# A depthwise 5x5 convolution on TensorE: stores issued by ACT, a reordered first channel, other waits on DVE

## The chip, the cores and the metric

One core of a Trainium2 chip runs the kernel. The metric is device time in microseconds (us) of one execution. The engines are TensorE (PE, with its weight loads shown as PEld), VectorE (DVE), ScalarE (ACT), GpSimd (POOL) and SyncE (SP). DMAs are issued here by SP and by ACT (their queues are shown as SPq and ACTq) and run on 16 DMA engines.

## The reference

The input x is 128 images of 55 x 55 pixels with 96 channels, float32. Each channel is convolved with its own 5 x 5 kernel, and the input is added:

```python
ch = x.shape[-1]
k = jnp.transpose(kernel, (1, 2, 0))[:, :, None, :]
y = lax.conv_general_dilated(x, k, window_strides=(1, 1), padding='SAME',
                             dimension_numbers=('NHWC', 'HWIO', 'NHWC'), feature_group_count=ch)
return x + y
```

Four of the 96 kernels are not zero in the given data, but the kernel computes all 96 alike.

## The kernel before, in words

**Layout.** The host turns x so that a channel is one array of 128 partitions by 3200 columns. The 55 x 55 image is cut into 5 x 5 squares of 11 x 11 pixels. Partition p is pixel p of a square (121 are used), and the columns run over strips (five columns of squares, j = 0 to 4), squares of a strip (top to bottom) and the 128 images. So one square of all images is a 121 x 128 block, and it is the stationary operand of a matmul. The moving operand is the channel's taps, spread out into a 121 x 225 matrix: from each of the 121 pixels to the 15 x 15 window that it reaches. The product, 128 images by up to 225 pixels, goes to PSUM. The 1 on the centre tap adds the input itself.

**Precision.** x and the taps are each split into a high part that TensorE takes exactly (float32r) and the rest. Three products make the result: x_low with the high taps, x_high with the high taps, x_high with the low taps. ACT makes x_high (`split_high`, L336 to L347, a copy with rounding), DVE or POOL subtracts to get x_low (`split_low`, L282 to L286). From channel 1 on, a channel is split in two pieces (LATER_PIECES, L116): strips 0 and 1, whose x_low DVE makes, and strips 2 to 4, whose x_low POOL makes. Channel 0 is split in five pieces, one a strip, all by DVE. The taps are split by DVE in batches of four channels, in three steps (`split_taps`, L243 to L268), and placed into the weights by one multiplication with a mask (`place_taps`, L270 to L280): by DVE for channel 0, by POOL for all others.

**Tiles.** A channel has 14 tiles (TILES, L60): in each of the strips 0 to 3 the squares (0), (1, 2) and (3, 4), in strip 4 the squares (0, 1) and (2, 3, 4). A tile has a PSUM bank of its own; there are 8, used in turn, so tile i waits until tile i - 8 is finished (`wait_bank`, L434 to L442; i runs on through the channels). A tile with one square (`alone`) takes two matmuls, since its third product is put beside the second in one instruction and lands in a part of the bank of its own. The others take three matmuls a square. That makes 71 matmuls in a channel.

**Finishing a tile.** Windows of neighbouring squares overlap by four pixels, the seam. ACT copies the pixels of a tile that no tile before has touched from PSUM to y_out (`copy_sums`, L349 to L354). DVE then adds what is left (`finish_sums`, L371 to L395): in an alone tile the low part of the same pixels (L381); where the tile has one above it, the four rows of seam (L386); where it has one to its left, the four columns of seam (L392), in an alone tile twice, for its high and its low part (L392, L395). Each addition counts up the semaphore y_step; `stepped(c, i)` is its value when tile i of channel c is done. Before L386 DVE waits until all steps of the tile before are complete (L384), and before L392 likewise (L391).

**Order on each engine.** The order is written out by hand. ACT (L356 to L367): issues the loads of start_in (the taps of channels 0 to 3, the unit kernel and the mask) and of the taps of batch 1, splits the five pieces of channel 0, then for each channel makes 14 copies, with the two splits of the next channel ahead of copies 0 and 3 (HIGH_AT, L119), in channel 0 ahead of copies 5 and 8. DVE (L397 to L420): zeroes the weights, splits and places the taps of channel 0, makes the five x_low of channel 0 with the taps of channels 1 to 3 split behind the second; then for each channel finishes the 14 tiles, with x_low of the next channel's first piece and, in three channels of four, one step of the next batch's taps ahead of tile 0 (in channel 0 ahead of tile 5). POOL (L424 to L430): for each channel from 1 on waits for DVE's x_low of that channel, places the taps, makes x_low of the second piece. PE (L487 to L500): 15 products of zeros, then for each channel waits for the weights and, at each piece, for its x_low, and computes the tiles. SP (L311 to L332): loads channel 0 in five pieces and channels 1 to 3 whole, then in iteration c loads channel c + 4 into one of four slots of x_in once both x_low of channel c are made, reloads taps in every fourth, waits for the last finish of channel c and stores the channel from one of four slots of y_out. So a store stands between two loads on SP's queue, and both go through it in order. The last channel is stored in five parts.

Of the kernel before, what the change touches and what calls it, by code (L numbers as in the profile page):

```python
# [15 lines left out]
P = 128  # L16
# [95 lines left out]
ZERO_PRODUCTS = 15  # L112
# [7 lines left out]
FIRST_HIGH_AT = (5, 8)  # L120

# [55 lines left out]
def build(nc, x, taps, start, out):  # L177
    with ExitStack() as ctx:  # L178
# [16 lines left out]
        start_in = sbuf("start_in", [P, (BATCH + 1) * TURNED_COLS + TAP_COLS], F32)  # L195
# [8 lines left out]
        first_loaded = sems("first_loaded", GRID)  # L204
        x_loaded = sems("x_loaded", X_SLOTS)
# [32 lines left out]
        def given_taps(batch):  # L238
            if batch == 0:
                return start_in[0:SQUARE, 0:BATCH * TURNED_COLS].rearrange("p (c n) -> p c n", n=TURNED_COLS)  # L240
            return taps_in[batch % TAPS_SLOTS][0:SQUARE, :, :]

        def split_taps(engine, batch, first, end, step):  # L243

            slot, count = batch % SPLIT_SLOTS, end - first
            given = given_taps(batch)[:, first:end, :]
            high, low = (taps_split[slot][0:SQUARE, first:end, part, :] for part in (HIGH, LOW))
            left = rest[slot][0:SQUARE, first:end, :]
            at = BATCH * TURNED_COLS
            centre = start_in[0:SQUARE, at:at + TURNED_COLS].unsqueeze(1).broadcast_to([SQUARE, count, TURNED_COLS])  # L250
            if step == 0:
                if batch == 0:
                    engine.wait_ge(start_loaded, 16)
                else:

                    slot_uses = uses(batch, TAPS_SLOTS) + (batch % TAPS_SLOTS > 0)
                    engine.wait_ge(taps_loaded[batch % TAPS_SLOTS], 16 * slot_uses)
# [12 lines left out]
        def place_taps(engine, c):  # L270
# [3 lines left out]
            mask = start_in[0:SQUARE, (BATCH + 1) * TURNED_COLS:].rearrange("p (a n) -> p a n", n=TURNED_COLS).unsqueeze(1).broadcast_to(shape)  # L274
# [16 lines left out]
        def _(sp):  # L291
# [22 lines left out]
            for c in range(1, X_SLOTS):  # L314
                load_x(c)
            sp.wait_ge(margins_zeroed, Y_SLOTS)
            for c in range(LAST):
# [4 lines left out]
                store_y(c)  # L322
# [12 lines left out]
        def _(act):  # L335
            def split_high(c, piece):  # L336
                cols = piece_cols(c, piece)
                if c == 0:
                    act.wait_ge(first_loaded[piece], 16)
                elif piece == 0:  # L340

                    act.wait_ge(x_loaded[c % X_SLOTS], 16 * (uses(c, X_SLOTS) + (c % X_SLOTS > 0)))
# [12 lines left out]

# [4 lines left out]
            for piece in range(len(pieces_of(0))):  # L360
                split_high(0, piece)
# [191 lines left out]
```

## Time and profile before

| | us |
|---|---|
| median of 3 runs (806.47 to 806.73) | 806.69 |
| the profiled execution, its own time | 806.57 |
| its span, first to last instruction | 804.8 |
| PE busy | 795.2 |
| DVE busy | 675.4 |
| ACT busy | 644.5 |
| POOL busy | 520.7 |

The kernel moves 313.41 MB at a mean of 389 GB/s. A span is the time between the first and the last instruction of the core; the time of an execution holds 1.8 us more. A row of a timeline has the start in us from the start of the span, the length in us, engine, line, operation, destination <- sources, and how often it follows itself without a gap; in brackets the idle time of the engine ahead of it and what ended that. Neighbouring steps of one engine overlap a little in these rows, since its pipeline takes the next one in before the last has drained. PE busy includes the time in which matmuls are pipelined.

### The profile page before, as it was taken

Reading aid. Unit: us, or ns where it says so; the run is one execution under the profiler, and the core shown is the slowest. Engines: PE = TensorE matmul, PEld = TensorE weight load, DVE = VectorE, ACT = ScalarE, POOL = GpSimd, SP = SyncE. Lnnn points to the kernel's source line nnn. Section 1 sums busy time; section 2 is a strip of 40 time slices with the busy share of each in tenths; the row PEclk is TensorE's granted clock in tenths of the full one; section 3 lists DMA queues with packets and bytes.
Section 4 is the critical chain, followed back from the end, with each engine's and each line's share of the span. In section 5 each row is a group of like instructions: output and inputs, shape, how many; then the busy total and the mean of one; then the engine's idle time right before and its main releaser. Section 6 shows DMA issues by size and latency. Waiting matters only on the chain.

```text
span 804.8 us, 20077 instructions
## 1 busy us (share of the span) xinstructions
PE 795.2 (99%) x6831; PEld 793.1 (99%) x6831; DVE 675.4 (84%) x2776; ACT 644.5 (80%) x1541; POOL 520.7 (65%) x194
## 2 busy tenths in 40 slices
PE   7999999999999999999999999999999999999997
PEld 7999999999999999999999999999999999999997
DVE  7888888888888888888888888888888888888886
ACT  6778888787878888787878788787878788787875
POOL 2675766667675767666675757666675757666672
PEclk9999999999999999999999999999999999999999
DMA  9999999999999999999999999999999999999975
GB/s 364 418 388 399 399 398 394 397 406 391 394 399 398 395 401 392 399 400 395 398 392 402 394 396 396 396 403 396 393 392 403 388 401 389 405 401 388 397 286 236
DMA packets 32358, 313.41 MB, mean 389 GB/s; under 512 B 3584, under 2 KB 6528, under 8 KB 7936
## 3 DMA queue, kind: packets, MB, share of 16 engines
q1 hardware_dynamic: 31968, 311.67, 97.9%
q8 instruction: 54, 0.88, 0.4%
q10 hardware_dynamic: 288, 0.46, 0.2%
q14 instruction: 48, 0.39, 0.1%
HBM read 161.13 MB, written 150.99 MB: 388 GB/s over the span
## 4 chain that ended last, share of the span: by engine, by line
PE 97%; DMA 1%; DVE 1%; SPq 0%; issue 0%; ACT 0%; DVEq 0%
PE sums L481 82%; PE sums L470 9%; PE sums L468 5%; DMA x_in<-x 1%; SPq L313 0%; DVE x_low L285 0%; DVE y_out L392 0%; DVE y_out L386 0%; ACT x_high L346 0%; DVE y_out L381 0%; DVE taps_split L262 0%; DVE y_out L395 0%; ACT y_out L354 0%; DVE rest L266 0%; DVEq L178 0%
## 5 line engine op out<-in xcount | busy, mean ns | idle before, releaser
L481 PE MATMUL sums<-weights,x_high 121*128 121x226 f32 (+3 forms) x4032 | 689.6, 275 | 0.0
L481 PEld LDWEIGHTS sums<-weights,x_high 121*128 121x128 f32 x4032 | 611.1, 192 | 0.0
L481 PE MATMUL sums<-weights,x_low 121*128 121x226 f32 (+3 forms) x2016 | 546.8, 271 | 1.8 <-DVE y_out L392 1.1
L354 ACT ACTIVATE y_out<-sums 128x242 f32<-128x242 f32 (+5 forms) x1344 | 389.6, 378 | 149.8 <-PE sums L481 149.7
L285 POOL TENSOR_TENSOR x_low<-x_in,x_high 121x1920 fp32r<-121x1920 f32 x95 | 411.5, 4332 | 0.0
L481 PEld LDWEIGHTS sums<-weights,x_low 121*128 121x128 f32 x2016 | 387.0, 192 | 2.3 <-DVE y_out L392 1.3
L346 ACT ACTIVATE x_high<-x_in 121x1920 fp32r<-121x1920 f32 (+1 forms) x195 | 298.0, 1528 | 5.0 <-DMA x_in<-x 4.8
L280 POOL TENSOR_TENSOR weights<-taps_split,start_in 121x450 fp32r<-121x450 f32 x95 | 113.0, 1189 | 271.7 <-DVE x_low L285 220.9
L392 DVE TENSOR_TENSOR y_out<-sums,y_out 128x96 f32<-128x96 f32 (+3 forms) x1056 | 258.3, 245 | 11.6 <-DVE y_out L386 1.3
L386 DVE TENSOR_TENSOR y_out<-sums,y_out 128x44 f32<-128x44 f32 (+2 forms) x864 | 177.1, 205 | 93.8 <-ACT y_out L354 3.7
L285 DVE TENSOR_TENSOR x_low<-x_in,x_high 121x1280 fp32r<-121x1280 f32 (+1 forms) x100 | 146.0, 1463 | 0.5 <-ACT x_high L346 0.5
L470 PE MATMUL sums<-weights,x_high 121*128 121x392 f32 (+1 forms) x384 | 140.0, 365 | 0.0
L381 DVE TENSOR_TENSOR y_out<-sums,y_out 128x143 f32<-128x143 f32 (+1 forms) x384 | 116.9, 304 | 5.6 <-ACT y_out L354 5.3
L468 PE MATMUL sums<-weights,x_low 121*128 121x196 f32 (+1 forms) x384 | 106.2, 277 | 2.4 <-DVE x_low L285 1.9
L468 PEld LDWEIGHTS sums<-weights,x_low 121*128 121x128 f32 x384 | 73.7, 192 | 2.9 <-DVE weights L280 2.3
L470 PEld LDWEIGHTS sums<-weights,x_high 121*128 121x128 f32 x384 | 73.7, 192 | 0.0
L395 DVE TENSOR_TENSOR y_out<-sums,y_out 128x52 f32<-128x52 f32 x288 | 61.3, 213 | 9.9
L266 DVE TENSOR_TENSOR rest<-taps_split,start_in 121x300 f32<-121x300 f32 (+2 forms) x25 | 11.3, 451 | 0.1
L262 DVE TENSOR_TENSOR taps_split<-taps_in,start_in 121x300 fp32r<-121x300 f32 x23 | 10.7, 465 | 0.0
L268 DVE TENSOR_TENSOR taps_split<-taps_in,rest 121x300 fp32r<-121x300 f32 x23 | 10.7, 463 | 0.0
L489 PE MATMUL sums<-zeros 128*128 128x512 f32 x15 | 5.1, 508 | 1.1 <-DVE zeros L397 1.1
L489 PEld LDWEIGHTS sums<-zeros 128*128 128x128 f32 x15 | 3.8, 261 | 1.9 <-DVE zeros L397 1.0
(13 smaller groups left out, 5.2 us busy)
## 6 DMA issues: line engine op xcount, KB each, us to landing
x_in<-x SPq DMA_DIRECT2D x95, 1600.0 KB, 12.6
y<-y_out SPq DMA_DIRECT2D x95, 1536.0 KB, 8.5
taps_in<-taps SPq DMA_DIRECT2D x22, 150.0 KB, 12.8
x_in<-x SPq DMA_DIRECT2D x5, 320.0 KB, 6.0
y<-y_out SPq DMA_DIRECT2D x3, 302.5 KB, 2.3
y<-y_out SPq DMA_DIRECT2D x1, 357.5 KB, 3.7
start_in<-start ACTq DMA_DIRECT2D x1, 300.0 KB, 4.9
y<-y_out SPq DMA_DIRECT2D x1, 271.0 KB, 2.4
```

The lines of the kernel that those rows point to most:

```text
L266: engine.tensor_tensor(left, high.bitcast(F32), centre, ALU.subtract).then_inc(taps_step, 1)
L280: engine.tensor_tensor(windows, turned, mask, ALU.mult).then_inc(weights_ready[slot], 1)
L285: engine.tensor_tensor(x_low[slot][0:SQUARE, cols], x_in[c % X_SLOTS][0:SQUARE, cols], x_high[slot][0:SQUARE, cols].bitcast(F32), ALU.subt ...
L346: act.activation(x_high[c % SLOTS][0:SQUARE, cols], x_in[c % X_SLOTS][0:SQUARE, cols], ACT.Copy).then_inc(high_ready[c % SLOTS], 1)
L354: act.activation(y, sums, ACT.Copy).then_inc(tile_copied, 1)
L381: dve.tensor_tensor(own, low_sums, own, ALU.add).then_inc(y_step, 1)
L386: dve.tensor_tensor(seam, sums[:, 0:SEAM, FRESH_AT[j]:FRESH_AT[j] + FRESH[j]], seam, ALU.add).then_inc(y_step, 1)
L392: dve.tensor_tensor(seam, sums[:, :, 0:SEAM], seam, ALU.add).then_inc(y_step, 1)
L395: dve.tensor_tensor(seam, sum_view(c, i, LOW)[:, :, 0:SEAM], seam, ALU.add).then_inc(y_step, 1)
L468: pe.matmul(sums[:, HIGH], x_low[slot][0:SQUARE, at:at + IMAGES], windows[:, HIGH], start=True, stop=False, skip_group_check=True)
L470: product = pe.matmul(sums, x_high[slot][0:SQUARE, at:at + IMAGES], windows, start=False, stop=True, skip_group_check=True)
L481: product = pe.matmul(sums, v[slot][0:SQUARE, at:at + IMAGES], window, start=n == 0 and v is x_low, stop=n == len(squares) - 1 and part == ...
```

## The change

1. The stores of whole channels leave SP. ACT issues them on its own queue: the store of channel c - 1 comes behind the fourth copy of channel c (STORE_AT = 3), after a wait for the last copy and the last step of DVE on channel c - 1. The five parts of the last channel stay on SP.
2. start_in holds the taps of channel 0 alone, with the unit kernel and the mask. Those of channels 1 to 3 come with a load of the whole batch 0 into taps_in, issued by ACT behind start_in.
3. Channel 1 is loaded in its two pieces, each with a semaphore of its own.
4. In the first strip of channel 0 TensorE first makes all products with x_high, then, after the wait for x_low, those with x_low. There are 17 products of zeros instead of 15.
5. POOL no longer waits for DVE's x_low of channel 1 before it places that channel's taps.
6. On DVE an alone tile adds the high part of its column seam first, then its own low part, then the low part of the seam. The wait before the row seam is gone unless the tile before is alone, and there it asks for the steps up to the tile's own pixels only.
7. ACT, not SP, waits for the margins of y_out to be zeroed, after its splits of channel 0.

The rest of the diff gives `tile` the new name `products` and lets it take a list of the products wanted; for all strips but the first of channel 0 their order is the same as before.

```diff
-ZERO_PRODUCTS = 15
+ZERO_PRODUCTS = 17
+STORE_AT = 3
...
-        start_in = sbuf("start_in", [P, (BATCH + 1) * TURNED_COLS + TAP_COLS], F32)
+        start_in = sbuf("start_in", [P, 2 * TURNED_COLS + TAP_COLS], F32)
...
+        second_loaded = sems("second_loaded", len(LATER_PIECES))
...
         @block.sync
...
-            def store_y(c):
-                sp.wait_ge(tile_copied, copied(c, LAST_TILE))
-                sp.wait_ge(y_step, stepped(c, LAST_TILE))
-                sp.dma_start(out[c, :, :], y_out[c % Y_SLOTS][:, :]).then_inc(y_stored[c % Y_SLOTS], 16)
-
             for j in range(GRID):
                 cols = piece_cols(0, j)
                 sp.dma_start(x_in[0][:, cols], x[0, :, cols]).then_inc(first_loaded[j], 16)
-            for c in range(1, X_SLOTS):
+            for piece in range(len(LATER_PIECES)):
+                cols = piece_cols(1, piece)
+                sp.dma_start(x_in[1][:, cols], x[1, :, cols]).then_inc(second_loaded[piece], 16)
+            for c in range(2, X_SLOTS):
                 load_x(c)
-            sp.wait_ge(margins_zeroed, Y_SLOTS)
             for c in range(LAST):
                 if c + X_SLOTS < CHANNELS:
                     load_x(c + X_SLOTS)
                 if c % BATCH == 0 and c // BATCH + BATCHES_AHEAD < BATCHES:
                     reload_taps(c // BATCH + BATCHES_AHEAD)
-                store_y(c)
...
         @block.scalar
...
+                elif c == 1:
+                    act.wait_ge(second_loaded[piece], 16)
...
+            def store_y(c):
+
+                act.wait_ge(tile_copied, copied(c, LAST_TILE))
+                act.wait_ge(y_step, stepped(c, LAST_TILE))
+                act.dma_start(out[c, :, :], y_out[c % Y_SLOTS][:, :]).then_inc(y_stored[c % Y_SLOTS], 16)
+
             act.dma_start(start_in[:, :], start).then_inc(start_loaded, 16)
+            load_taps(act, 0)
             load_taps(act, 1)
...
+            act.wait_ge(margins_zeroed, Y_SLOTS)
             for c in range(CHANNELS):
                 places = HIGH_AT if c else FIRST_HIGH_AT
                 for i in range(len(TILES)):
                     if i in places and c < LAST:
                         split_high(c + 1, places.index(i))
                     copy_sums(c, i)
+                    if i == STORE_AT and c > 0:
+
+                        store_y(c - 1)
...
         @block.vector
...
                 dve.wait_ge(tile_copied, copied(c, i))
                 if alone(i):
                     own, low_sums = fresh(c, i, LOW)
+                    if col_seam(i):
+
+                        seam = y_view(c, j - 1)[:, first:end, FRESH[j - 1] - SEAM:FRESH[j - 1]]
+                        dve.wait_ge(y_step, stepped(c, i - 1) - col_seam(i - 1))
+                        dve.tensor_tensor(seam, sums[:, :, 0:SEAM], seam, ALU.add).then_inc(y_step, 1)
                     dve.tensor_tensor(own, low_sums, own, ALU.add).then_inc(y_step, 1)
+                    if col_seam(i):
+                        dve.wait_ge(y_step, stepped(c, i - 1) + 1)
+                        dve.tensor_tensor(seam, sum_view(c, i, LOW)[:, :, 0:SEAM], seam, ALU.add).then_inc(y_step, 1)
+                    return
                 if row_seam(i):
-
-                    dve.wait_ge(y_step, stepped(c, i - 1))
+                    if alone(i - 1):
+
+                        dve.wait_ge(y_step, stepped(c, i - 2) + 1 + col_seam(i) if i > 1 else stepped(c, 0))
...
-                    if alone(i):
-                        dve.wait_ge(y_step, stepped(c, i) - 1)
-                        dve.tensor_tensor(seam, sum_view(c, i, LOW)[:, :, 0:SEAM], seam, ALU.add).then_inc(y_step, 1)
...
         @block.gpsimd
...
             for c in range(1, CHANNELS):
-
-                pool.wait_ge(low_by_dve[c % SLOTS], lows(c, 0))
+                if c > 1:
+
+                    pool.wait_ge(low_by_dve[c % SLOTS], lows(c, 0))
                 place_taps(pool, c)
                 split_low(pool, c, 1, low_by_pool)
...
         @block.tensor
...
+                by_low, by_high = ((x_low, HIGH),), ((x_high, HIGH), (x_high, LOW))
                 for piece, (first, end) in enumerate(pieces_of(c)):
-
                     low_ready = low_by_dve if by_dve(c, piece) else low_by_pool
+                    tiles = [i for i in range(len(TILES)) if first <= TILES[i][0] < end]
+                    if (c, piece) == (0, 0):
+
+                        pe.wait_ge(high_ready[slot], highs(c, piece))
+                        for i in tiles:
+                            products(c, i, by_high, True, False)
+                        pe.wait_ge(low_ready[slot], lows(c, piece))
+                        for i in tiles:
+                            products(c, i, by_low, False, True)
+                        continue
+
                     pe.wait_ge(low_ready[slot], lows(c, piece))
-                    for i in range(len(TILES)):
-                        if first <= TILES[i][0] < end:
-                            tile(c, i)
+                    for i in tiles:
+                        wait_bank(c, i)
+                        products(c, i, by_low + by_high, True, True)
```

## Rows read from the trace of the kernel before

**Rows 1.** The page, busy time, share and instructions of each engine.
```profile
PE 795.2 (99%) x6831; PEld 793.1 (99%) x6831; DVE 675.4 (84%) x2776; ACT 644.5 (80%) x1541; POOL 520.7 (65%) x194
```

**Rows 2.** Windows: busy us (instructions) of PE, PEld, DVE, ACT, POOL; clock, DMA share, GB/s.
```profile
10.00:20.00 10.00, 8.93 (x76) 8.74 (x75) 8.60 (x30) 8.18 (x21) 3.83 (x2) 1.00 1.00 424
30.00:785.00 755.00, 755.00 (x6524) 754.85 (x6523) 640.06 (x2641) 613.25 (x1470) 504.23 (x184) 1.00 1.00 394
...
708.00:709.00 1.00, 1.00 (x12) 1.00 (x11) 0.76 (x5) 0.57 (x2) 1.00 (x1) 1.00 0.96 295
```

**Rows 3.** Waits of PE: who waited for whom, us in total, times, longest us.
```profile
PE sums L481 <- DVE y_out L392: 1.1, 1, 1.1
```

**Rows 4.** Timeline of all engines, 0 to 8.3 us.
```profile
1.05 5.11 PE L489 MATMUL sums<-zeros 128*128 128x512 f32 x15 [1.05 <-DVE zeros L397]
...
5.76 0.24 DVE L262 TENSOR_TENSOR taps_split<-start_in 121x75 fp32r<-121x75 f32 x1 [3.45 <-DMA start_in<-start]
...
7.12 1.55 DVE L285 TENSOR_TENSOR x_low<-x_in,x_high 121x640 fp32r<-121x640 f32 x2
...
8.08 0.33 PE L468 MATMUL sums<-weights,x_low 121*128 121x182 f32 x1 [1.92 <-DVE x_low L285]
```

**Rows 5.** Timeline of DVE, 13 to 21 us.
```profile
13.28 0.21 DVE L395 TENSOR_TENSOR y_out<-sums,y_out 128x52 f32<-128x52 f32 x1
13.60 0.20 DVE L386 TENSOR_TENSOR y_out<-sums,y_out 128x44 f32<-128x44 f32 x1
13.72 0.26 DVE L392 TENSOR_TENSOR y_out<-sums,y_out 128x104 f32<-128x104 f32 x1
14.44 1.49 DVE L285 TENSOR_TENSOR x_low<-x_in,x_high 121x1280 fp32r<-121x1280 f32 x1 [0.46 <-ACT x_high L346]
15.85 0.46 DVE L262 TENSOR_TENSOR taps_split<-taps_in,start_in 121x300 fp32r<-121x300 f32 x1
...
16.34 0.24 DVE L392 TENSOR_TENSOR y_out<-sums,y_out 128x96 f32<-128x96 f32 x1
...
20.49 2.40 DVE L285 TENSOR_TENSOR x_low<-x_in,x_high 121x1280 fp32r<-121x1280 f32 x1
```

**Rows 6.** Timeline of PE, 18 to 40 us, its last row with a wait.
```profile
23.57 0.37 PE L481 MATMUL sums<-weights,x_low 121*128 121x226 f32 x1 [0.76 <-DVE y_out L381]
```

**Rows 7.** Timeline of ACT and of POOL, 9 to 20 us.
```profile
9.93 1.38 ACT L354 ACTIVATE y_out<-sums 128x169 f32<-128x169 f32 x5
13.13 1.27 ACT L346 ACTIVATE x_high<-x_in 121x1280 fp32r<-121x1280 f32 x1 [1.82 <-DMA x_in<-x]
...
14.96 1.82 ACT L346 ACTIVATE x_high<-x_in 121x1920 fp32r<-121x1920 f32 x1
...
17.20 4.34 POOL L285 TENSOR_TENSOR x_low<-x_in,x_high 121x1920 fp32r<-121x1920 f32 x1
```

**Rows 8.** Timeline in channel 94: ACT's copies, DVE's last step on the fifth tile, TensorE's tile 12.
```profile
788.00 1.69 ACT L354 ACTIVATE y_out<-sums 128x143 f32<-128x143 f32 x7
...
789.24 0.26 DVE L392 TENSOR_TENSOR y_out<-sums,y_out 128x104 f32<-128x104 f32 x1
...
790.34 0.19 PEld L481 LDWEIGHTS sums<-weights,x_low 121*128 121x128 f32 x1
```

**Rows 9.** DMA issues (ns min/median/max); landing of stores; landing of x loads from 600 us.
```profile
L235 SPq DMA_DIRECT2D taps_in<-taps x22: 428/953/2112, 12.5 to 704.5; - x22
L235 ACTq DMA_DIRECT2D taps_in<-taps x1: 457/457/457, 1.2 to 1.2; - x1
...
y<-y_out SPq DMA_DIRECT2D x95, 1536.0 KB, 8.5
...
DMA to landing us min/median/max: 12.2/12.8/13.7
```

**Rows 10.** The end: timeline of ACT in the last channel, and one window.
```profile
793.94 0.60 ACT L354 ACTIVATE y_out<-sums 128x260 f32<-128x260 f32 x2 [0.25 <-PE sums L481]
...
800.00:802.00 2.00, 0.48 (x5) 0.31 (x3) 0.58 (x3) 0.40 (x1) 0.00 (x0) 1.00 0.54 208
```

More of the change, by code:

```diff
@@ L442, in wait_bank, with products @@
                     pe.wait_ge(tile_copied, copied(c + back, before))
-            def tile(c, i):
+            def products(c, i, kinds, starts, stops):
                 j, squares = TILES[i]
@@ L447, in tile @@
                 first_col, cols = SUM_COLS[j]
-                wait_bank(c, i)
                 for n, square in enumerate(squares):
@@ L458, in tile @@
                     run = lead + count + (lead + count) % 2
-                    if alone(i):
-                        if cols == WINDOW:
-                            windows = weights[slot][0:SQUARE, :, origin:origin + run]
-                            sums = psum[:, bank_of(c, i), 0:2 * run].rearrange("p (w n) -> p w n", w=2)
-                        else:
-                            windows = weights[slot][0:SQUARE, :, origin:origin + (end - first) * WINDOW].rearrange(
-                                "p w (r c) -> p w r c", c=WINDOW)[:, :, :, first_col:first_col + cols]
-                            sums = psum[:, bank_of(c, i), 0:2 * run].rearrange("p (w r c) -> p w r c", w=2, c=cols)
-                        pe.matmul(sums[:, HIGH], x_low[slot][0:SQUARE, at:at + IMAGES], windows[:, HIGH],
-                                  start=True, stop=False, skip_group_check=True)
-                        product = pe.matmul(sums, x_high[slot][0:SQUARE, at:at + IMAGES], windows,
-                                            start=False, stop=True, skip_group_check=True)
-                        break
@@ L473, in tile @@
-                    for v, part in ((x_low, HIGH), (x_high, HIGH), (x_high, LOW)):
-                        if cols == WINDOW:
-                            window = weights[slot][0:SQUARE, part, origin - lead:origin - lead + run]
-                            sums = psum[:, bank_of(c, i), to - lead:to - lead + run]
-                        else:
-                            window = weights[slot][0:SQUARE, part, origin:origin + (end - first) * WINDOW].rearrange(
-                                "p (r c) -> p r c", c=WINDOW)[:, :, first_col:first_col + cols]
-                            sums = psum[:, bank_of(c, i), to:to + count].rearrange("p (r c) -> p r c", c=cols)
-                        product = pe.matmul(sums, v[slot][0:SQUARE, at:at + IMAGES], window,
-                                            start=n == 0 and v is x_low,
-                                            stop=n == len(squares) - 1 and part == LOW, skip_group_check=True)
@@ L484, in tile @@
-                product.then_inc(tile_summed, 1)
+                    if cols == WINDOW:
+                        windows = weights[slot][0:SQUARE, :, origin - lead:origin - lead + run]
+                        sums = psum[:, bank_of(c, i), to - lead:to - lead + run]
+                        both = psum[:, bank_of(c, i), 0:2 * run].rearrange("p (w n) -> p w n", w=2)
+                    else:
+                        windows = weights[slot][0:SQUARE, :, origin:origin + (end - first) * WINDOW].rearrange(
+                            "p w (r c) -> p w r c", c=WINDOW)[:, :, :, first_col:first_col + cols]
+                        sums = psum[:, bank_of(c, i), to:to + count].rearrange("p (r c) -> p r c", c=cols)
+                        both = psum[:, bank_of(c, i), 0:2 * run].rearrange("p (w r c) -> p w r c", w=2, c=cols)
@@ new lines, in products @@
+                    for v, part in kinds:
+                        ends = {"start": starts and n == 0 and (v, part) == kinds[0],
+                                "stop": stops and n == len(squares) - 1 and (v, part) == kinds[-1]}
+                        pixels = v[slot][0:SQUARE, at:at + IMAGES]
+                        if alone(i) and part == LOW:
+                            continue
+                        if alone(i) and v is x_high:
+                            ends["stop"] = stops and kinds[-1][0] is x_high
+                            product = pe.matmul(both, pixels, windows, skip_group_check=True, **ends)
+                        else:
+                            product = pe.matmul(sums, pixels, windows[:, part], skip_group_check=True, **ends)
@@ L487, in _ @@
+                if stops:
+                    product.then_inc(tile_summed, 1)
             pe.wait_ge(zeros_ready, 1)
```

23 lines of the change are left out of this document (10 added, 13 removed).

## The prediction

> **What bounds the kernel now.** The page first: TensorE is busy for 795.2 of 804.8 us, over 6831 matmuls, of which 15 are the warm-up products on zeros, so a channel has 71 [rows 1]. Then the long middle: from 30 to 785 us TensorE is busy all 755.00 us, 6524 matmuls, 8.22 us a channel; in the same stretch the DMA engines show a busy share of 1.00 at 394 GB/s [rows 2]. So nothing outside TensorE can shorten the middle, and a slower transfer rate could lengthen it. What can be won lies at the two ends. Third the waits of TensorE: 1.1 us for a seam addition of DVE (L392) [rows 3], before it 1.9 us for the first x_low [rows 4], after it 0.8 us for the addition at L381 [rows 6]. All fall before 24 us. The timelines of that stretch tell who is late: the first product starts at 8.08 [rows 4]; DVE then works without a break from 14.44 on [rows 5], and TensorE waits for it for the last time, until 23.57 [rows 6]. The whole run after 23.57 is TensorE's, so **the gain is the amount by which 23.57 moves**.
>
> **Start of the first channel.** The weights are placed by DVE in the four steps that begin when start_in lands, at 5.76; x_low follows at 7.12 and TensorE starts 8.08 [rows 4]. start_in shrinks from 300 to 188 KB. It shares the engines with x, which moves as much in the same time, so I give it 0.3 us (bounds: 0, and 0.5, 112 KB twice over at the 424 GB/s of the loads from 10 to 20 us [rows 2]). Since the first strip's products with x_high now come first, TensorE needs only the weights, ready as x_low starts: 7.12 - 0.3 + 0.1 = about 7.0 instead of 8.08. The two more zero products cost nothing: 15 take 5.11 us, at most 0.34 each, and end at 6.16, so 17 end by 6.84 [rows 4]. The low products of the strip come 1.0 us later, after their x_low (7.9 - 0.3 = 7.6). This gains 1.1 us at the start, but not at the end of the chain, as DVE is what is late next.
>
> **DVE in the first channel.** It was late by its own work, then by 0.46 us waiting for x_high of channel 1, whose load landed at 13.13 [rows 5, 7]. With the load in two parts the first part lands 983 KB earlier, 2.3 us at 424 GB/s: 10.8 us, so ACT splits it right after its first five copies, at 11.3, done by 12.6. DVE's own work before that shifts by the 0.28 us of start_in. The new waits: start to start, the step behind a dependent one costs 0.32 (13.28 to 13.60), an independent one 0.12 (13.60 to 13.72) [rows 5]. A strip has three such places; I take 0.35 us a strip (bounds 0.1 and 0.5). DVE's five finishes left the engine free at 13.72 + 0.26, less the 0.08 by which steps overlap (14.44 + 1.49 against 15.85), 13.90; now 13.90 - 0.28 - 0.35 = 13.27: x_low of channel 1 runs 13.27 to 14.75, the taps' step 14.68 to 15.14 (1.41 later, as 14.44 to 15.85), and the seam that frees TensorE's bank, 16.34 to 16.58 before, ends at 15.41 [rows 5]. TensorE took 7.5 us from its first product to that wait (it resumed at 16.6, behind the seam, having waited 1.1 [rows 3]), so it arrives at 14.6 (the split of the third strip, ready at 10.3, holds it up by 0.1), waits to 15.5, and is 1.1 us ahead.
>
> **POOL, the next late one.** Its x_low of channel 1 (4.34 us) ran 17.20 to 21.54 [rows 7]. DVE's x_low of channel 2 started inside it, at 20.49, and took 2.40 us where the same shape takes 1.49 [rows 5]: it ended 1.35 us after POOL did, although it started 1.05 before. So DVE does not get through while POOL subtracts, and the end of POOL's step sets the end of DVE's. POOL no longer waits for DVE before it places the weights of channel 1 (1.1 us, now about 10 to 13 us); its x_low then waits for ACT's x_high alone. ACT's split of the second part was 14.96 to 16.78 [rows 7]. The new one starts when the load has landed, 13.13 + 0.1 for 38 KB more in front, 13.2; the work before it (five copies from 9.93 to 11.31, the first part's split of 1.27, three copies at 0.28) is done by 13.2 too [rows 7]. x_high is ready at 15.05, POOL runs 15.15 to 19.49. DVE, which came to its x_low of channel 2 at 20.49, now comes 1.17 + 3 x 0.35 earlier, at 18.3, so earlier inside POOL's step, and has it done at 19.49 + 1.35 = 20.84 instead of 22.89, so **2.05 us earlier**. Then one step of taps and the first finish: the release of 23.57 comes at 21.5. TensorE itself would be there at 15.5 + 1.1 + 4.2 = 20.8 (9 products of channel 0's last tile, 36 of channel 1's 71), so it still waits for DVE, and the chain's gain stands: 2.0 us. Its bounds: 1.05, if DVE is a microsecond later in all this (below), and 2.8, where TensorE's own work ends it.
>
> **The stores on ACT's queue.** What is queued behind the issue on ACT: copies 5 to 10 of the channel, which DVE and then TensorE's banks wait for. In channel 94 ACT is behind: its copies run back to back from 788.00, 0.24 each; DVE's work on the fifth ends 789.50, and TensorE needs it at 790.34 [rows 8]. The trace shows ACT issuing a small transfer in 0.46 us; SP's reloads of taps, behind others in its queue, took 0.43 to 2.11 us, median 0.95 [rows 9]. I take 0.45 us, the nearest case (same engine, one transfer ahead): it eats half of the 0.84 us in hand, and DVE's shorter waits give part of it back. Cost nothing; gone is that cover from about 1.3 us on. Its two waits, for copies and seams of the channel before, are long met. SP's loads and taps no longer stand behind a store: the load for channel c+4 goes out as soon as POOL's x_low of channel c ends, and nobody waits for it. A slot of y_out is stored behind the fourth copy of the next channel and written again 2.5 channels later, 20 us; a store lands in 8.5 [rows 9]: nothing. The margins' zeros, for which ACT now waits before its first copy, are an early step of DVE; the taps of channels 1 to 3 come in a load of their own on ACT's queue, second in it, and are wanted at 8.3, well after start_in, which is first: nothing either.
>
> **The end.** The last full store goes out behind the fourth copy of the last channel, 793.94 + 0.6 [rows 10], 0.6 us later than before. But the engines stood at 208 GB/s from 800 to 802, half of the 424 that they reach [rows 2, 10], so 1 us of the queue was free before the last strips' stores went out. Nothing (bound: 0.3 us).
>
> **Sum** against the profiled execution: 806.57 (span 804.8) - 2.0 = 804.6; the median of the runs is 0.12 higher: **804.7 us**, 0.25% faster. What a measurement of this kernel can tell from no change is about 0.2%, 1.6 us.
>
> **A rule against it.** The rows show one case, DVE held up by POOL, which had begun first [rows 5, 7]. The Trainium skill, page "SBUF — State Buffer" (Practical consequences), says that a VectorE instruction with two SBUF inputs contends with a GpSimd one that reads SBUF, and whichever issues first holds the port for its whole duration. By that rule the order in which they come decides, which is the first rival.
>
> **Rival 1, POOL comes first (11%).** DVE's taps step starts at 14.68 by my sum, POOL's x_low at 15.15: 0.45 us between them. If DVE is later than that, the step stands behind 4.34 us of POOL: its start goes to 19.5, the seam to 20.2, so TensorE resumes at 20.3 instead of 16.64, and with 1.1 + 4.2 us of products up to the place of 23.57 is there at 25.6: 2.0 us slower, 808.7; with POOL's placing also ahead of two DVE splits, 809.3. For it: POOL's placing now comes at about 9.7, amid DVE's splits, where its 1.07 us may push them back. Against: DVE is then queued back to back. If only that microsecond is lost, and DVE keeps its turn (14%), POOL starts 1 us later too: 805.7.
>
> **Rival 2, the transfers slow down (12%).** Loads and stores stood in one queue; now they are mixed on two. The engines have no idle share to lose [rows 2]. A load takes up to 13.7 us to land late in the run [rows 9] against three channels, 24.6: 11 us in hand. Over 755 us a rate 1.5% lower uses that up; 3% is 22.7 us, less the 11: 816. The slowest microsecond, at a change from loads to stores, had 295 GB/s [rows 2]: mixing may cost, or cost no more than now. The Trainium skill ("DMA: Bandwidth & Descriptors", Issuing engines are not separate DMA queues) has all issuers share the same 16 engines and interleave; by it no rate is won, and none need be lost.
>
> **Rival 3, the issue on ACT (4%).** At 2.1 us each, 0.8 us of TensorE wait in 94 channels: 880. **Rival 4, nothing late but TensorE (4%)**: 2.8 us, 803.9. The forecast has the rest, 55%, alone 804.0 to 805.5.
>
> **Chances.** Faster takes four fifths of the forecast, rival 4 and a little of the rest: 0.50. Within 0.2%: the fifth, the lost microsecond, half of a mild rival 2: 0.29. Slower: 0.21. The range 803.9 to 808.8 holds all but the dearer part of rivals 1, 2 and 3.
>
> **What would show it.** First product at 7.0; POOL's x_low of channel 1 starting near 15.15, with DVE's taps step ahead of it; last TensorE wait ending near 21.5; 8.22 us a channel after. DVE's x_low(2) still at 2.4 us or more. I am wrong if a TensorE wait appears beyond 30 us, if ACT's store issues exceed 1.3 us, or if a DVE step without POOL's size takes over 4 us.

## The result, and the profile after

The changed kernel takes **809.96 us** (median of 5 runs, 809.51 to 810.89) against 806.6 for the kernel before: a ratio of 1.0044, 95% interval 1.0033 to 1.0055. It is 3.4 us slower. The forecast was 804.7 us, with a range of 803.9 to 808.8.

From the page of the changed kernel its span, the busy times, and the issues of loads and stores (the last figure of a row is the median time in us from issue to landing; line numbers are those of the changed kernel: L282 is `split_low`, L259 the first step of `split_taps`, L277 `place_taps`, L341 `split_high`, L349 `copy_sums`, L355 the store, L493 and L491 the matmuls; in the versions below they shift by a few lines):

```profile
span 808.1 us, 19890 instructions
PE 796.8 (99%) x6833; PEld 795.0 (98%) x6833; DVE 631.3 (78%) x2776; ACT 644.8 (80%) x1541; POOL 522.1 (65%) x194
...
x_in<-x SPq DMA_DIRECT2D x94, 1600.0 KB, 11.4
y<-y_out ACTq DMA_DIRECT2D x95, 1536.0 KB, 11.2
```

DVE is busy 44 us less than before (675.4 in [rows 1]) and the span is 3.3 us longer: where DVE's time was saved it was not the bound. TensorE has two waits beyond its start, and the timeline of TensorE, 3 to 40 us, shows where:

```profile
12.39 0.38 PE L493 MATMUL sums<-weights,x_low 121*128 121x226 f32 x1 [1.40 <-DVE y_out L392]
...
19.93 0.54 PE L493 MATMUL sums<-weights,x_low 121*128 121x210 f32 x1 [4.31 <-DVE y_out L408]
...
24.88 0.36 PE L491 MATMUL sums<-weights,x_high 121*128 121x392 f32 x1
```

The wait of 4.31 us is the one that was 1.1 us in [rows 3]. Why DVE was so late stands in its timeline and in POOL's:

```profile
8.90 3.19 DVE L282 TENSOR_TENSOR x_low<-x_in,x_high 121x640 fp32r<-121x640 f32 x3
...
13.70 1.48 DVE L282 TENSOR_TENSOR x_low<-x_in,x_high 121x1280 fp32r<-121x1280 f32 x1
15.10 4.51 DVE L259 TENSOR_TENSOR taps_split<-taps_in,start_in 121x300 fp32r<-121x300 f32 x1
...
9.16 1.52 POOL L277 TENSOR_TENSOR weights<-taps_split,start_in 121x450 fp32r<-121x450 f32 x1 [8.72 <-DVE taps_split L265]
14.72 4.55 POOL L282 TENSOR_TENSOR x_low<-x_in,x_high 121x1920 fp32r<-121x1920 f32 x1 [4.05 <-ACT x_high L341]
```

A step of taps that took 0.46 us in [rows 5] takes 4.51 here. It begins 0.38 us after POOL's x_low and ends 0.34 us after it: it stood behind POOL for the whole of POOL's instruction. The same happened in small before that: POOL's placing came in among DVE's last three splits, which took 2.29 us before and 3.19 now. Then the clock. These are windows of the changed kernel:

```profile
15.00:17.70 2.70, 0.63 (x6) 0.44 (x4) 2.70 (x2) 0.92 (x4) 2.70 (x1) 0.98 1.03 436
17.70:24.40 6.70, 4.46 (x20) 4.47 (x21) 5.72 (x21) 2.15 (x4) 1.57 (x1) 0.50 1.01 421
24.40:27.00 2.60, 2.60 (x24) 2.60 (x23) 1.84 (x5) 2.06 (x4) 1.22 (x1) 0.99 1.01 422
```

TensorE idled from 15.6 to 19.93. From 17.7 the granted clock is 0.50, that is 1.2 instead of 2.4 GHz, and it is back at full only near 24.4, so TensorE's first 4.5 us of work after the wait ran at half speed.

**Where the 3.7 us up to the third channel went.** The wide x_high product of an alone tile (L470 before, L491 after) is a marker in both traces. Between markers, after less before: up to tile 3 of channel 0, 9.87 and 8.23: 1.64 gained. From there to tile 9, 3.33 and 5.03: 1.70 lost, of which 1.40 is the first wait (its end, 12.39, is set by DVE: in the version a1 below TensorE arrives later and waits 0.58 us, until 12.49). From there to the resumption behind the seam, 3.44 and 6.67: 3.23 lost. From the resumption to tile 3 of channel 1, 2.83 and 4.95: 2.12 lost, with no wait recorded in it: the clock. From there to channel 2, 8.27 and 6.58: 1.69 gained, since the two later waits of the kernel before have nothing left to wait for. The sum is 3.72 lost. The middle gives 0.64 of it back (below), the end of this execution takes 0.2: 3.3.

### The profile page after: what moved, and what is told of

It reads as the page before. It is cut to its first block, busy times and chain, and to the rows that moved or that the text cites. A ratio compares the mean times of both kernels' runs of the same rounds, so it can differ in the third digit from the quotient of the medians.

```text
span 808.1 us, 19890 instructions
## 1 busy us (share of the span) xinstructions
PE 796.8 (99%) x6833; PEld 795.0 (98%) x6833; DVE 631.3 (78%) x2776; ACT 644.8 (80%) x1541; POOL 522.1 (65%) x194
## 4 chain that ended last, share of the span: by engine, by line
PE 97%; DVE 2%; DMA 1%; issue 0%; ACT 0%; DVEq 0%
PE sums L493 87%; PE sums L491 10%; DVE x_low L282 1%; DVE taps_split L259 1%; DMA start_in<-start 1%; DVE y_out L402 0%; DVE rest L263 0%; DVE taps_split L265 0%; DVE weights L277 0%; DVE y_out L392 0%; ACT y_out L349 0%; DVE y_out L408 0%; DVE y_out L391 0%; DVEq L180 0%; DVE y_out L395 0%
## 5 line engine op out<-in xcount | busy, mean ns | idle before, releaser
L493 PE MATMUL sums<-weights,x_high 121*128 121x226 f32 (+3 forms) x4032 | 690.5, 275 | 0.0
L493 PE MATMUL sums<-weights,x_low 121*128 121x226 f32 (+3 forms) x2400 | 652.6, 272 | 5.7 <-DVE y_out L408 4.3
L493 PEld LDWEIGHTS sums<-weights,x_high 121*128 121x128 f32 x4032 | 612.4, 192 | 0.0
L349 ACT ACTIVATE y_out<-sums 128x242 f32<-128x242 f32 (+5 forms) x1344 | 390.0, 378 | 154.6 <-PE sums L493 154.0
L493 PEld LDWEIGHTS sums<-weights,x_low 121*128 121x128 f32 x2400 | 461.4, 192 | 6.1 <-DVE y_out L408 4.5
L282 POOL TENSOR_TENSOR x_low<-x_in,x_high 121x1920 fp32r<-121x1920 f32 x95 | 411.9, 4335 | 4.6 <-ACT x_high L341 4.6
L341 ACT ACTIVATE x_high<-x_in 121x1920 fp32r<-121x1920 f32 (+1 forms) x195 | 298.0, 1528 | 2.4 <-DMA x_in<-x 2.2
L277 POOL TENSOR_TENSOR weights<-taps_split,start_in 121x450 fp32r<-121x450 f32 x95 | 114.1, 1201 | 268.8 <-DVE x_low L282 251.8
L402 DVE TENSOR_TENSOR y_out<-sums,y_out 128x44 f32<-128x44 f32 (+2 forms) x864 | 165.2, 200 | 65.5 <-ACT y_out L349 54.7
L408 DVE TENSOR_TENSOR y_out<-sums,y_out 128x96 f32<-128x96 f32 (+2 forms) x768 | 201.7, 263 | 11.3 <-DVE y_out L408 0.9
L282 DVE TENSOR_TENSOR x_low<-x_in,x_high 121x1280 fp32r<-121x1280 f32 (+1 forms) x100 | 146.5, 1467 | 71.1 <-ACT x_high L341 71.1
L491 PE MATMUL sums<-weights,x_high 121*128 121x392 f32 (+1 forms) x384 | 140.2, 365 | 0.0
L391 DVE TENSOR_TENSOR y_out<-sums,y_out 128x52 f32<-128x52 f32 x288 | 61.7, 214 | 21.2 <-ACT y_out L349 14.1
L491 PEld LDWEIGHTS sums<-weights,x_high 121*128 121x128 f32 x384 | 73.9, 192 | 0.3 <-DVE weights L277 0.3
L395 DVE TENSOR_TENSOR y_out<-sums,y_out 128x52 f32<-128x52 f32 x288 | 58.7, 204 | 0.0
L259 DVE TENSOR_TENSOR taps_split<-taps_in,start_in 121x300 fp32r<-121x300 f32 (+1 forms) x24 | 15.2, 633 | 0.0
L265 DVE TENSOR_TENSOR taps_split<-taps_in,rest 121x300 fp32r<-121x300 f32 (+1 forms) x24 | 11.1, 461 | 0.0
## 6 DMA issues: line engine op xcount, KB each, us to landing
x_in<-x SPq DMA_DIRECT2D x94, 1600.0 KB, 11.4
y<-y_out ACTq DMA_DIRECT2D x95, 1536.0 KB, 11.2
```

Of the source, the lines that this page charges most:

```text
L259: engine.tensor_tensor(high, given, centre, ALU.add).then_inc(taps_step, 1)
L277: engine.tensor_tensor(windows, turned, mask, ALU.mult).then_inc(weights_ready[slot], 1)
L282: engine.tensor_tensor(x_low[slot][0:SQUARE, cols], x_in[c % X_SLOTS][0:SQUARE, cols], x_high[slot][0:SQUARE, cols].bitcast(F32), ALU.subt ...
L341: act.activation(x_high[c % SLOTS][0:SQUARE, cols], x_in[c % X_SLOTS][0:SQUARE, cols], ACT.Copy).then_inc(high_ready[c % SLOTS], 1)
L349: act.activation(y, sums, ACT.Copy).then_inc(tile_copied, 1)
L391: dve.tensor_tensor(seam, sums[:, :, 0:SEAM], seam, ALU.add).then_inc(y_step, 1)
```

## The experiments

The theory, P: POOL's x_low of channel 1 and DVE's taps step, each with two operands in SBUF, exclude each other; POOL now comes first; TensorE waits 4.3 us and its clock falls. The rivals: the stores on ACT's queue (S), DVE's new order, the missing wait of POOL by itself. A ratio is to the kernel before, timed on the same chip; in brackets stands its 95% interval. Parts 2 and 4 of the change, the smaller start_in and the new order in the first strip, were not tried apart.

### Is it the stores?

Both ways round: the changed kernel with its stores back on SP's queue, and the kernel before with its stores on ACT's.

```diff
 a1, on ACT and on SP:
-                    if i == STORE_AT and c > 0:
-
-                        store_y(c - 1)
...
+                store_y(c)
 a2: the same the other way round
```

> The changed kernel with the stores back on SP's queue, all else as changed. Theory P (POOL's x_low of channel 1 takes the SBUF port ahead of DVE's taps step, TensorE idles 4.3 us and its granted clock falls to half until about 24.4 us): the start does not touch the stores, so the stall of 4.31 us and the slow stretch are still there and the time stays at 809.5 to 810.5 us. Rival S (the stores on ACT's queue cost the time, through ACT's issue or the mixed transfers): back at 806.6 us or below, since what is left of the change only works before 25 us.

> The kernel before with its stores on ACT behind the fourth copy and nothing else changed. Theory P: no change within the measurement, 806.3 to 807.3 us, 8.22 us a channel, no wait of TensorE beyond 30 us. Rival S: the loss of 3.3 us shows here, 809 to 811 us.

Measured: 810.52 us, ratio 1.0045 (1.0033 to 1.0058), and 806.63 us, ratio 0.9999 (0.9990 to 1.0008). With the stores on SP the loss is all there; with the stores on ACT alone there is none. **S falls, and the part that gave the change its name moves nothing.** In the changed kernel the loads land in 11.4 us and the stores in 11.2, against 12.6 and 8.5 before: the two share the engines now instead of queueing. The kernel before with ACT's stores (a2) has the same rate in the middle as without them:

```profile
30.00:785.00 755.00, 755.00 (x6523) 754.83 (x6522) 640.32 (x2641) 613.12 (x1469) 504.12 (x184) 1.00 1.00 394
```

What the issue costs ACT is seen in the same kernel's timeline of ACT and its queue:

```profile
785.96 0.34 ACTq L355 DMA_DIRECT2D y<-y_out  x1
...
787.86 1.69 ACT L349 ACTIVATE y_out<-sums 128x143 f32<-128x143 f32 x7
```

The program puts the store behind the fourth copy. It is issued at 785.96, while that copy starts at 787.86: ACT's instructions are handed to it ahead of their execution, and the issue passes by the side. The seven copies take 1.69 us, as in [rows 8]. The issue costs ACT nothing, and the store leaves nearly when it did on SP. The Trainium skill, page "Perfetto Trace Analysis" (DVE / Act Engine Instruction), has the sequencer push such an instruction into a wait queue and go on to decode the next. By that rule, the trace agrees: 1.9 us ahead of the copy.

### Is it POOL's missing wait, and which part of it?

Three edits of POOL's part for channel 1 in the changed kernel: the old wait restored; only the x_low held until DVE's taps step is done; only the placing held until DVE's splits of channel 0 are done.

```diff
 a3:
-                if c > 1:
-                    pool.wait_ge(low_by_dve[c % SLOTS], lows(c, 0))
+                pool.wait_ge(low_by_dve[c % SLOTS], lows(c, 0))
 a4:
                 place_taps(pool, c)
+                if c == 1:
+                    pool.wait_ge(taps_step, split_steps(c) + 1)
 b1:
                 if c > 1:
                     pool.wait_ge(low_by_dve[c % SLOTS], lows(c, 0))
+                else:
+                    pool.wait_ge(low_by_dve[0], lows(0, GRID - 1))
```

> The changed kernel, where POOL waits again for DVE's x_low of channel 1 before it places that channel's taps. Theory P: DVE's five first splits are free of POOL (2.3 us for the last three, not 3.19), its taps step is ahead of POOL's x_low, which runs about 15.5 to 19.9 us; the granted clock stays at full; DVE's x_low of channel 2 ends near 21.3 and TensorE's last wait near 21.9: 804.9 us (804.3 to 805.7). Rival D (DVE's new order of steps or the earlier start itself makes the stall): still 808 us or more.

> The changed kernel, where POOL still places the taps of channel 1 early, amid DVE's splits, but its x_low of channel 1 waits for DVE's taps step. Theory P (it is the order of those two at the port that costs, not the early placing): the splits are still 3.2 us and TensorE still waits 1.4 us near 12.4, but DVE's taps step is 0.46 us, POOL's x_low runs 15.6 to 20.0, full clock, last wait of TensorE ends near 21.9: 804.4 us (804.0 to 805.0), as with POOL's old wait. Rival E (the early placing makes the loss, as it puts DVE 0.9 us back): 806 us or more.

> The changed kernel, where POOL waits for DVE's last x_low of channel 0 before it places the taps of channel 1, so the placing is clear of DVE's splits, but its x_low is bound by nothing of channel 1 on DVE. Theory P: DVE is 0.9 us earlier than in the changed kernel, so its taps step begins near 14.2, ahead of POOL's request at 14.7; POOL runs 14.7 to 19.1, the last wait of TensorE ends near 21.1, full clock: 804.2 us (803.7 to 805.2). If the order at the port is not what decides (rival: DVE gives way whenever POOL wants the port), the 4.5 us step and the stall stay and the time is 808 us or more.

Measured: 804.37 us, ratio 0.9972 (0.9961 to 0.9982); 804.46 us, 0.9973 (0.9962 to 0.9984); 803.49 us, 0.9960 (0.9946 to 0.9974). All three lose the long step, keep the full clock, and are **faster than both kernels**. a3 and a4 fell within their forecasts, b1 0.2 us below its own. In a4 the early placing is there, the three splits take 3.20 us, and nothing is lost at the end against a3: where POOL's x_low is held back, the placing is harmless. What costs is the order of x_low and taps step. But the early placing is what brings that order about: in b1 POOL's x_low is as free as in the changed kernel, only the placing comes later, and DVE's taps step starts 1.0 us earlier (14.06 against 15.10) and is ahead. The version b1 has the order that I had forecast, and its timeline of DVE and POOL shows the taps step ahead:

```profile
14.06 0.47 DVE L259 TENSOR_TENSOR taps_split<-taps_in,start_in 121x300 fp32r<-121x300 f32 x1
17.84 2.42 DVE L282 TENSOR_TENSOR x_low<-x_in,x_high 121x1280 fp32r<-121x1280 f32 x1
...
14.58 4.34 POOL L282 TENSOR_TENSOR x_low<-x_in,x_high 121x1920 fp32r<-121x1920 f32 x1 [2.18 <-ACT x_high L341]
...
20.95 0.37 PE L495 MATMUL sums<-weights,x_low 121*128 121x226 f32 x1 [0.59 <-DVE y_out L392]
```

The last wait ends at 20.95, as POOL's x_low moved from 17.20 to 14.58. The distance from b1 to the changed kernel is 6.5 us, and it hangs on which of the two steps is asked for first, by 0.4 us.

### Does it need the earlier load as well?

The kernel before with only POOL's wait taken away, and the changed kernel with channel 1 loaded whole.

```diff
 d1:
-            for piece in range(len(LATER_PIECES)):
-                cols = piece_cols(1, piece)
-                sp.dma_start(x_in[1][:, cols], x[1, :, cols]).then_inc(second_loaded[piece], 16)
+            sp.dma_start(x_in[1][:, :], x[1, :, :]).then_inc(second_loaded[0], 16)
```

> The kernel before with only POOL's wait for DVE's x_low of channel 1 taken away. Theory P: x_high of channel 1's second piece is ready only at 16.8 here, and DVE, 0.9 us later than it was, starts its taps step about 16.2, ahead of POOL: no long step, no stall of 4 us, full clock, 806.2 to 807.0 us; so the part is harmless without the earlier load of channel 1. Rival D (taking the wait away is a loss by itself, because DVE then always stands behind POOL): 809 us or more.

> The changed kernel with channel 1 loaded whole, as before, POOL's missing wait left as changed. Theory P (POOL's x_low and DVE's taps step meet only because the load in two pieces lets ACT make the second x_high early): x_high of that piece is ready at 16.5, DVE's taps step begins about 15.6, ahead of it, and takes 0.47 us; full clock; last wait of TensorE near 23: 805.3 to 806.2 us. Rival (the missing wait alone makes POOL come first): 809 us or more.

Measured: 806.32 us, ratio 0.9996 (0.9987 to 1.0005), and 805.23 us, 0.9981 (0.9972 to 0.9991). The first has no measurable change, the second a gain. Neither shows a long step. In d1, DVE and POOL:

```profile
15.39 0.47 DVE L259 TENSOR_TENSOR taps_split<-taps_in,start_in 121x300 fp32r<-121x300 f32 x1
...
16.40 4.35 POOL L282 TENSOR_TENSOR x_low<-x_in,x_high 121x1920 fp32r<-121x1920 f32 x1 [5.80 <-ACT x_high L339]
```

POOL's x_high comes 1.7 us later than in the changed kernel and the taps step is past. So the loss needs two parts of the change together: the load in pieces, which makes x_high early, and the missing wait, which lets POOL use it at once and, by the early placing, puts DVE back. Take either away and there is no loss. That these two parts alone make it, without the rest of the change, was not run.

### Held for one instruction? And what does the clock cost?

POOL's x_low of channel 1 in two instructions. In c1 the cut is after strip 3, so the first has two thirds of the columns; the text recorded for it says half, wrongly. In c2 the cut is after strip 2, one third.

```diff
+                if c == 1:
+                    pool.wait_ge(high_ready[1], highs(1, 1))
+                    for first, end in ((2, 4), (4, GRID)):      # c2: ((2, 3), (3, GRID))
+                        cols = slice(first * STRIP_COLS, end * STRIP_COLS)
+                        half = pool.tensor_tensor(x_low[1][0:SQUARE, cols], x_in[1][0:SQUARE, cols],
+                                                  x_high[1][0:SQUARE, cols].bitcast(F32), ALU.subtract)
+                    half.then_inc(low_by_pool[1], 1)
+                    continue
```

> The changed kernel, with POOL's x_low of channel 1 cut into two instructions of half the length. Theory P, with the port held for one instruction and given to the engine that waits: DVE's taps step, which took 4.5 us, takes 2.3 to 2.8 us, the stall of TensorE 2.1 to 2.6 us, its clock does not fall or less long, POOL's second half ends about 19.8; 805.3 to 806.5 us. Rival (POOL holds the port as long as it has work queued): the step stays 4.5 us and the time 809.5 to 810.5 us.

> The changed kernel, with POOL's x_low of channel 1 cut 1 to 2 (strip 2 first, then strips 3 and 4; the cut before it was 2 to 1, and the DVE step fell from 4.5 to 3.2 us but the clock still fell). POOL's first part ends near 16.4, DVE's taps step takes about 1.7 us, TensorE waits 1.3 to 1.6 us. Theory P with the clock: a wait that short leaves the granted clock at full, so both the wait (4.31 us) and the slow stretch go: 804.0 to 805.0 us, a fall of about 5 us for 3 us less of waiting. Rival (the slow stretch costs little, the wait is nearly all): the fall is 3 us at most, 806.5 to 807.5 us.

Measured: 809.15 us, ratio 1.0027 (1.0016 to 1.0038), and 805.02 us, 0.9986 (0.9977 to 0.9995). The taps step in c1, then in c2:

```profile
15.20 3.16 DVE L259 TENSOR_TENSOR taps_split<-taps_in,start_in 121x300 fp32r<-121x300 f32 x1
```

```profile
15.27 1.81 DVE L259 TENSOR_TENSOR taps_split<-taps_in,start_in 121x300 fp32r<-121x300 f32 x1
```

4.51, 3.16, 1.81 us for a first instruction of 3, 2 and 1 strips: 1.35 us less a strip, and POOL's own pace is 4.34 / 3 = 1.45. The step waits for the instruction in front, not for POOL's queue; that rival falls. The time of c1 was missed by 2.7 us. The wait had fallen by 1.35 us, to 2.96, and the time by 0.8 only, since the clock fell all the same, from about 18.0 to 24.8, and TensorE worked for 6.1 us of that stretch (from 18.69 on), against 4.5 in the changed kernel.

How much of a slow stretch falls on work is not fixed by the wait. In a1, with the same wait of 4.31 us (15.7 to 20.03), the clock stayed at full until TensorE resumed, and then was at half until about 26.9:

```profile
15.80:20.00 4.20, 0.00 (x0) 0.00 (x0) 4.20 (x4) 0.31 (x1) 3.57 (x1) 1.00 0.99 421
20.10:26.80 6.70, 6.70 (x31) 6.70 (x31) 5.25 (x22) 3.60 (x6) 1.21 (x1) 0.50 0.96 394
```

All 6.8 us of it fell on work, and the profiled execution of a1 took 810.89 us where that of the changed kernel took 809.90. So the price of the clock, 2.1 us in the trace of the changed kernel, is not a constant. The runs of c1 fall apart likewise: five took 809.0 to 809.5 us at a mean granted clock of 0.995, two 807.8 at 0.997. In c2, with a wait of 1.61 us, most runs kept it, and the runs that did not give its price within one kernel: seven of 11 had a mean granted clock of 0.999 and 804.77 to 805.03 us, three had 0.997 or 0.998 and 806.5 to 806.6, one had 0.995 and 808.12. The dearest run is **3.1 us above the median, in one kernel**, more than the wait of 1.6 us itself; those runs left no trace, so that the clock is all of it is inferred. In the traces: from the changed kernel to c2 the wait is 2.7 us shorter and the time 4.9, and 2.12 us of the difference is the slow stretch measured above.

### What are DVE's new waits worth?

The kernel before with DVE's part of the change alone (new order and new waits, which were not tried apart), and b1 with DVE's old part.

> The kernel before with only DVE's new order and waits. Two things are asked. In the chain before 24 us: DVE's work in the free stretch shortens by about 0.2 us a strip, TensorE's last wait is still set by POOL's x_low of channel 1, so it moves by 0.2 to 0.4 us. In the middle: the changed kernel and its variants show 6528 to 6530 matmuls from 30 to 785 us, where the two kernels with DVE's old waits show 6523 and 6524; if DVE's waits are the cause (theory W), this kernel has 6528 or more and wins 0.6 us there, 805.7 us in all; if the earlier loads or another part is (rival), it has 6524 and 806.4 us.

> The version with POOL's placing behind DVE's last x_low of channel 0 (803.49 us), with DVE's old order and waits. It asks what those waits are worth there. In the middle the old waits cost 0.6 us. At the start DVE is 0.3 us later, so its taps step begins near 14.4, still ahead of POOL's request at 14.6: no long step, 804.1 to 804.8 us. If DVE is late enough to lose the port (rival, 0.2 us of room), the stall of 4.3 us and the slow stretch are back: 809 us or more.

Measured: 805.85 us, ratio 0.9991 (0.9982 to 1.0000), and 804.47 us, 0.9971 (0.9960 to 0.9983), which is 1.0 us above b1. In the middle, b3:

```profile
30.00:785.00 755.00, 755.00 (x6529) 755.00 (x6528) 593.84 (x2644) 613.85 (x1471) 504.65 (x184) 1.00 0.99 394
```

6529 products against 6524 in [rows 2], 5 x 116 ns = 0.6 us. The distances from channel to channel tell where they were lost: the kernel before has 8.21 or 8.22 us in nearly all channels, but 8.31 to 8.36 in five late ones and 8.23 to 8.25 in four others; the changed kernel has 8.21 or 8.22 in every one. Each is too short a stop to be shown as a wait. b1 has 6528 products there, and e1, with DVE's old part, 6523 again. In e1 the port is not lost (its taps step starts at 14.56, POOL's x_low at 14.84, with 0.28 us between), and the other 0.4 us are at the start: TensorE's last wait ends at 21.34 against 20.95.

### A version that beats both

In b1, DVE came to its x_low of channel 2 at 17.84 and stood 1.1 us behind POOL; the finish of tile 0, for which TensorE waited 0.59 us, was queued behind it.

```diff
-                    if i == (HIGH_AT if c else FIRST_HIGH_AT)[0]:
+                    if i == (3 if c == 1 else (HIGH_AT if c else FIRST_HIGH_AT)[0]):
```

> The version with POOL's placing behind DVE's last x_low of channel 0 (803.49 us), where in addition DVE makes x_low of channel 2 and the taps step behind tile 2 of channel 1 and not ahead of tile 0. In that version DVE stood 1.1 us behind POOL there and TensorE waited 0.59 us for the finish of tile 0. Theory P: DVE finishes tiles 0 to 2 while POOL has the port, since these additions have only one operand in SBUF, then finds the port free; the 0.59 us go, 802.9 us (802.6 to 803.3). Rival: DVE's later x_low pushes POOL's next placing and x_low and the wait comes back elsewhere: 803.5 us or more.

Measured: **802.65 us**, ratio 0.9949 (0.9936 to 0.9961). DVE's x_low, with the port free:

```profile
19.01 1.48 DVE L282 TENSOR_TENSOR x_low<-x_in,x_high 121x1280 fp32r<-121x1280 f32 x1
```

TensorE's last wait is now 0.27 us at 14.82. The 0.6 us of the wait went, and 0.2 more, whose source is open.

## Why the prediction was wrong, point by point

- **What bounds the kernel** was right: after the start all is TensorE's. That nothing outside TensorE could shorten the middle was wrong by 0.6 us: its busy time there was full, and still DVE held it up for some hundredths or a tenth of a us in nine channels.
- **Start of the first channel**: right in kind, too small. The load of start_in landed 0.85 us earlier, not 0.3 (4.91 against 5.76), and the first product came at 6.41, not 7.0.
- **DVE in the first channel**: the shorter waits were put at 0.35 us a strip, and the stretch of five finishes fell from 2.03 us (11.95 to 13.98 in the timeline of before) to 1.77 (12.02 to 13.79): 0.26.
- **POOL, the next late one: this is the step that failed.** It has DVE's taps step start at 14.68 and POOL's x_low at 15.15. They started at 15.10 and 14.72. Each side was off by 0.4 us, in opposite directions. ACT's second x_high started at 12.83, not 13.2. DVE was 0.4 us late: POOL's placing took 0.9 us of it and the shorter waits gave 0.1 less than put, while the start was 0.6 us earlier than put. The sum had no term for the placing and named it only under rival 1. So the path was wrong: DVE's taps step stood behind POOL for 4.51 us instead of passing ahead of it in 0.46. With the order as forecast, as in b1, the rest of the sum holds, too cautious: the last wait is over at 20.95 where it said 21.5, since POOL's x_low started at 14.58 and not 15.15, and the time is 803.49 us where it said 804.7; the other 0.6 is the middle.
- **Rival 1** had the mechanism, its place and its point of decision, with 11%, and 809.3 us with the placing in front. Its price lacked the clock, 2.1 us. Against that, 1.4 us of the price did not come: the middle gave 0.6, TensorE resumed at 19.93 and not 20.3, and the 0.6 that it added for the placing was not lost, since POOL's x_low, which sets the end of the stall, waits only for ACT; the end of the trace took 0.2 back. So the time fell 1.2 us beyond the range. Two starts that lie 0.45 us apart, each the sum of five or six estimated terms, are a coin toss, not 11%.
- **The stores on ACT's queue**: nothing was right as the cost, the working was not: the issue was to delay the copies by 0.45 us and delays them by none.
- **The end**: nothing was forecast, and this stands. From the start of the last copy to the end it is 4.28 us before and 4.5 in the trace of the changed kernel, but 4.2 in those of a3, a4, b1 and d2, whose end is the same program: the 0.2 is of that one execution.
- **Rivals 2 and 3** fell with the two runs that moved the stores alone. **Rival 4** did not come either: in b1 TensorE still waits for DVE, until 20.95.

## What to carry to other kernels

Where a port or lock is held for a whole instruction, the length of an instruction is the price of coming second, and an earlier transfer or a dropped wait can turn the order round: before making a long step of one engine start sooner, list what the other engine does at that time with the same port, and keep an explicit wait unless the distance is larger than the error of the estimate. A stop of TensorE is to be priced with its clock, and as a range, since here the same stop cost 1 us more or less by when the clock fell. And moving DMA issues from one queue to another is worth trying on the chip alone before it is bundled with anything else.

## What the runs showed of the hardware that was not expected

- **The waiting engine gets the port ahead of the next in line.** POOL's x_low was asked for at 14.72, while DVE's split (13.70 to 15.18) still ran; DVE's next step followed without a gap and yet stood behind POOL. POOL's placing at 9.16 likewise came in between two splits of DVE that are issued back to back; its row is 1.52 us against 1.07, so it waited 0.45 for the first. The Trainium skill, page "SBUF — State Buffer" (Practical consequences), says that issue order decides who blocks. By that rule, the trace agrees: the request made first won, at 9.16 and at 14.72, although DVE had the port at both times. c1 and c2 show it the other way round: DVE's taps step, waiting behind POOL's first instruction, was done at 18.36 in c1, 1.4 us before POOL's second instruction, next in POOL's queue, ended at 19.75. That it is the time of the request that counts is my reading of these rows and was not varied by itself.
- **Additions with one operand in PSUM pass.** In d2 DVE's finishes run at their usual 0.2 to 0.3 us while POOL holds the port from 14.55 to 18.88.
- **The clock fell at different times in the same stop.** In the changed kernel it fell 2.1 us into the idle stretch of 4.3 (0.81 in the window from 17 to 18 us, 0.50 from 18 on) and stayed at half for 4.5 us of work; in a1 it fell only as TensorE resumed, and stayed at half for 6.8 us of work. In c1, with a wait of 2.96 us, it fell too; in the trace of c2, with 1.61 us, it did not. In the kernel before, TensorE stood 1.92 us in [rows 4] and the granted clock did not fall.
- **Loads and stores on two queues** moved the same 394 GB/s as on one.
